# Delta rule: ScalarE issues the transfers of the inverted diagonal blocks, the sync engine only those of the key blocks

## The reference

```python
def step(S, inputs):
    q_t, k_t, v_t, g_t, b_t = inputs
    S = S * jnp.exp(g_t)[..., None, None]
    kv = jnp.einsum('bhk,bhkv->bhv', k_t, S)
    u = b_t[..., None] * (v_t - kv)
    S = S + jnp.einsum('bhk,bhv->bhkv', k_t, u)
    o_t = jnp.einsum('bhk,bhkv->bhv', q_t * scale, S)
    return (S, o_t)
...
_, o = jax.lax.scan(step, S0, (tfirst(q), tfirst(k), tfirst(v), tfirst(g), tfirst(beta)))
...
x = x + _L0_attn_ref(_layernorm(x, axis=-1), ...)
x = x + _L0_ffn_ref(...)
x = x + _L1_attn_ref(...)
x = x + _L1_ffn_ref(...)
```

## Time and profile before

| | |
|---|---|
| median of 3 runs | 2797.41 us (2793.74 to 2800.77) |
| the profiled execution's own time | 2793.88 us |
| its span in the trace | 2792.1 us |
| mean granted clock of TensorE | 0.972 |
| TensorE busy | 94% of the span |
| ScalarE busy | 32% |
| GpSimd busy | 14% |
| the main loop of the delta rule | about 244 to 560 us of the span, a round every 41 to 43 us |

### The profile page before, as it was taken

The page is one execution under the profiler, slowest core; times in us unless marked ns, Lnnn a source line. Parts: engine busy times, 40 slices in busy tenths (PEclk is TensorE's granted clock), DMA queues, the critical chain, the costliest instruction groups (busy, mean ns, idle before and its releaser), DMA issues. The chain is left out here.

```text
span 2792.1 us, 34293 instructions
## 1 busy us (share of the span) xinstructions
PE 2624.4 (94%) x12650; PEld 1956.9 (70%) x12650; DVE 1636.0 (59%) x2426; ACT 886.6 (32%) x1354; POOL 389.1 (14%) x676
## 2 busy tenths in 40 slices
PE   8964889789999999999999989999999989999998
PEld 7844777768888888888888864333333678888886
DVE  7873777574544444455444477777776465655554
ACT  3342443232111111111211125666665322222221
POOL 0018877400000000000000022222210100000000
PEclk9977999989999999999999998999999999999999
DMA  2341331211100000000000014222221000100001
GB/s 92 110 122 41 86 82 40 63 36 33 31 24 23 23 23 23 23 23 23 23 23 23 1 44 76 71 70 72 72 79 37 31 16 32 45 31 15 15 16 46
DMA packets 104218, 122.32 MB, mean 44 GB/s; under 512 B 47454, under 2 KB 80478, under 8 KB 102438
## 3 DMA queue, kind: packets, MB, share of 16 engines
q1 hardware_dynamic: 104102, 120.79, 15.2%
HBM read 88.26 MB, written 24.64 MB: 40 GB/s over the span
## 5 line engine op out<-in xcount | busy, mean ns | idle before, releaser
L2236 DVE TENSOR_REDUCE att_top<-att_scores 128x1 f32<-128x1024 f32 x256 | 312.3, 1224 | 129.3 <-PE att_scores L2396 129.2
L296 DVE TENSOR_TENSOR fp_hidden<-fp_gelu,fp_up 128x512 f32<-128x512 f32 x128 | 88.0, 688 | 440.5 <-PE fp_up L75 377.5
L2109 ACT ACTIVATE att_probs<-att_scores 128x1024 f32<-128x1024 f32 x256 | 262.1, 1024 | 190.5 <-PE att_scores L2421 188.7
L2436 PE MATMUL att_out<-att_probs,att_padded 128*64 128x512 f32 x1024 | 269.5, 616 | 3.0 <-issue 2.8
L278 DVE TENSOR_TENSOR k_stream<-k_stream,fp_down 128x512 f32<-128x512 f32 x256 | 175.2, 685 | 84.1 <-PE fp_down L75 80.7
L356 ACT ACTIVATE fp_gelu<-fp_gate 128x512 f32<-128x512 f32 x128 | 76.3, 596 | 419.7 <-PE fp_gate L75 418.9
L73 PE MATMUL fp_gate<-fp_feat_hi,fp_w_hi 128*128 128x512 f32 x512 | 200.4, 391 | 4.6 <-DVE fp_feat_lo L266 4.6
L75 PE MATMUL fp_gate<-fp_feat_hi,fp_w_lo 128*128 128x512 f32 x512 | 199.9, 391 | 0.0
L74 PE MATMUL fp_gate<-fp_feat_lo,fp_w_hi 128*128 128x512 f32 x512 | 199.9, 390 | 0.0
L73 PE MATMUL fp_down<-fp_w_hi,fp_h_hi 128*128 128x512 f32 x512 | 199.3, 389 | 0.0
L75 PE MATMUL fp_up<-fp_feat_hi,fp_w_lo 128*128 128x512 f32 x512 | 199.2, 389 | 0.0
(11 more groups left out here) (336 smaller groups left out, 5560.5 us busy)
## 6 DMA issues: line engine op xcount, KB each, us to landing
f_early<-codes SPq DMA_DIRECT2D x16, 768.0 KB
f_early<-scales SPq DMA_DIRECT2D x16, 768.0 KB
att_stacks<-rotated SPq DMA_DIRECT2D x96, 128.0 KB
la_values<-w_sparse SPq DMA_DIRECT2D x10, 1024.0 KB, 4.8
f_early<-qkv SPq DMA_DIRECT2D x14, 576.0 KB, 5.6
att_stacks<-rotated SPq DMA_DIRECT2D x96, 64.0 KB
k_stream<-hidden SPq DMA_DIRECT2D x16, 256.0 KB, 4.2
att_stacks<-att_rot_hi SPq DMA_DIRECT2D x64, 64.0 KB
```

Of the source, the lines that this page charges most:

```text
L296: dve.tensor_tensor(hidden[:, c, :], gelu[:, c, :], up_ps[c][:], ALU.mult).then_inc(product_done, 1)
L2109: act.activation(probs[:, tile % PROBS, :], key_bank(tile)[:], ACT.Exp).then_inc(exp_done, 1)
L2236: dve.tensor_reduce(top[g % 2][:, STACK + t:STACK + t + 1], query_bank(tile)[:], AX.XY, ALU.max, negate=True).then_inc(max_done, 1)
L2436: last = pe.matmul(out[rows, :], padded[:, g % 2, t, :], probs[:, t, half * TB:(half + 1) * TB], start=t == 0, stop=t == T - 1)
```

## The change

SP no longer has `give_blocks`; it keeps `take_blocks`, the loads, and `start_base`. The ten DMAs of `give_blocks` stand in ScalarE's queue, at two places: the store of `base_t`, the four into `diag`, and the store of `base_tt` where `turn_blocks(c + 1)` stood (behind `square_outputs(c)`), and the four into `diag_t` behind `copy_off_blocks(c, 2)` of the round that uses them. Sizes, number and kinds of the DMAs stay. `start_base(c + 3)` on SP now waits for the store of chunk c + 1 and for its transposition, nothing else.

```diff
-            def give_blocks(c):
-                sp.wait_ge(zero_done, 3)
-                for base, produced, scratch, out, target, read, done in (
-                        (base_t, base_done, blocks_t, t_out, diag, m_ps, diag_in),
-                        (base_tt, tt_done, blocks_tt, tt_out, diag_t, y_ps, diag_t_in)):
-                    sp.wait_ge(produced, c + 1)
-                    if c:
-                        sp.wait_ge(done, 16 * QUARTERS * c)
-                    sp.dma_start(scratch.rearrange("q i r c -> (q i) r c"), base[base_rows(c), :, :]).then_inc(out, 16)
-                    sp.wait_ge(out, 16 * (c + 1))
-                    if c:
-                        sp.wait_ge(read, FOURS * c)
-                    for q in range(QUARTERS):
-                        at = slice(BASE * q, BASE * (q + 1))
-                        sp.dma_start(target[at, :, at], scratch[q].rearrange("i r c -> r i c")).then_inc(done, 16)
-                if c + 2 < CHUNKS:
-                    start_base(c + 2)
-
...
-            give_blocks(0)
+            sp.wait_ge(t_out, 16)
+            sp.wait_ge(tt_done, 1)
+            start_base(2)
...
-                if c + 1 < CHUNKS:
-                    give_blocks(c + 1)
+                if c + 3 < CHUNKS:
+                    sp.wait_ge(t_out, 16 * (c + 2))
+                    sp.wait_ge(tt_done, c + 2)
+                    start_base(c + 3)
...
+            def take_inverse(c, base, produced, scratch, out, done):
+                act.wait_ge(produced, c + 1)
+                if c:
+                    act.wait_ge(done, 16 * QUARTERS * c)
+                act.dma_start(scratch.rearrange("q i r c -> (q i) r c"), base[base_rows(c), :, :]).then_inc(out, 16)
+
+            def place_inverse(c, scratch, out, target, read, done):
+                act.wait_ge(out, 16 * (c + 1))
+                if c:
+                    act.wait_ge(read, FOURS * c)
+                for q in range(QUARTERS):
+                    at = slice(BASE * q, BASE * (q + 1))
+                    act.dma_start(target[at, :, at], scratch[q].rearrange("i r c -> r i c")).then_inc(done, 16)
+
+            def give_blocks(c):
+                take_inverse(c, base_t, base_done, blocks_t, t_out, diag_in)
+                turn_blocks(c)
+                place_inverse(c, blocks_t, t_out, diag, m_ps, diag_in)
+                take_inverse(c, base_tt, tt_done, blocks_tt, tt_out, diag_t_in)
+
...
-            turn_blocks(0)
+            act.wait_ge(zero_done, 3)
+            give_blocks(0)
...
                 copy_off_blocks(c, 2)
+                place_inverse(c, blocks_tt, tt_out, diag_t, y_ps, diag_t_in)
                 if ahead:
                     square_keys(ahead)
...
                     square_outputs(c)
-                    turn_blocks(c + 1)
+                    give_blocks(c + 1)
```

## The result

The changed kernel takes 2838.25 us (median of 5 runs, 2836.47 to 2839.96), before 2797.41 (5 runs, 2793.54 to 2800.77): a ratio of 1.015, 95% interval 1.0136 to 1.0164, or 41 us slower. The forecast was 2817 us with a range of 2805 to 2826. The direction was right, the size half of what came, and the time lies above the range.

What follows compares the result with a forecast made beforehand. The landing of diag, awaited by TensorE's off_blocks, was taken as the bound. Terms 9.8 + 2.5 + 1.4 + 5.3 + 0.7 = 19.7 us, added to the 2797.41 us median, gave 2817 us; range for 8 in 10: 2805 to 2826 us.

Steps and rivals of the forecast that it cites:

- late store, chunks 1 to 5: Before off_blocks of chunks 1 to 5: ScalarE stores the inverses later than SP did, 9.8 us together.
- What bounds the kernel: In the delta rule, TensorE's off_blocks waits for the DMAs into diag, 23.0 us over chunks 1 to 7.
- The store behind `square_outputs`: ScalarE's queue: store 0.05 us after the second square starts, placing 2.48 later, off_blocks 3.65 after that; 9.8 us in all.
- the rival with issues of 0.05 us: "Not slower": ScalarE issues DMAs in a fraction of SP's 0.46 us; about +4 us, 2801 us; chance 0.12.
- What SP does earlier: Unit matrix and load issued beside the DMAs into diag: 1.0 us each before chunks 0 to 4, 0.3 for chunk 5; 5.3 us.
- the upper bound of 2.5 us: Most that SP's transfers could delay the DMAs into diag per round, from a 512 KB residual landing in 5.0 against 2.5 us.
- much slower: Placing DMAs wait for the load (12.5 us), ScalarE's DMAs for its engine's work (4.5 us): 31 us, 2829 us; chance 0.08.
- The DMAs into `diag_t`: Ahead of square_keys on ScalarE, they delay the squares: 2.5 us over rounds 1 to 5, 1.4 us in round 0.
- The clock: Before chunk 3, TensorE's off_blocks would start at half clock after the longer wait: at most 1.5 us, taken as 0.7.
- the cover for which I took half: ScalarE's copies run beside off_blocks' half-clock products, so only half of at most 1.5 us was counted, 0.7 us.
- The lateness of chunk 6: About 2 us, expected to disappear in TensorE's 8.81 us wait for GpSimd before chunk 7.
- `square_queries` behind the placing DMAs: On ScalarE, square_queries starts 2.3 us later but has cover: costed at nothing, up to 2.3 us in five rounds without it.

Runs made afterwards that it cites:

- e1: Changed kernel, but SP waits until the four DMAs into diag have landed before issuing the unit matrix and the load; 2811.68 us, ratio 1.0059.
- e5: Changed kernel with only the four DMAs into diag_t moved behind square_keys; 2835.59 us, ratio 1.0145.
- e4: Kernel before, with only the store of base_tt and the four DMAs into diag_t issued by ScalarE; 2804.4 us, ratio 1.0034.
- e9: e1 with the store of base_t moved in front of square_outputs; 2796.64 us, ratio 0.9999.
- e11: e6 with 24 extra products in front of TensorE's wait for diag in every round but the first; 2808.35 us, ratio 1.0044.
- e7: Kernel before, all on SP, with the store of base_t in front of the wait for the key blocks' landing; 2792.69 us, ratio 0.9981.
- e10: Kernel before, with only the store of base_t on ScalarE, behind copy_queries and in front of square_outputs; 2791.57 us, ratio 0.9989.
- e12: e6 with 12 extra products in front of TensorE's wait for diag; 2804.13 us, ratio 1.0037.
- e6: e1 with the four DMAs into diag_t moved from in front of square_keys to behind it; 2809.17 us, ratio 1.0045.

## Why the forecast was half the size

Its terms against what the runs gave, for rounds 0 to 5:

| term | forecast | measured | from |
|---|---|---|---|
| late store, chunks 1 to 5 | 9.8 | 9.75 | e1 against before |
| the DMAs into `diag` beside SP's transfers | 5.3 | 26 | after against e1 |
| `diag_t` ahead of the squares of the keys | 3.9 | 5.3 | round 0: 3.9, of which 1.6 at half clock; round 1: about 1.4 (40.3 against 38.9 in e5) |
| half clock behind the longer waits | 0.7 | 5 | what is left of the 6.4 of rounds 1 to 5 without that 1.4 |
| sum | 19.7 | 46 | 45.6 in the spans |

**What bounds the kernel.** Right: the landing of `diag` was on the path, and 31.5 of 45.6 us appear in that wait.

**The store behind `square_outputs`.** Right in each step, and in the lead of the sequencer over the engine. ScalarE issues a DMA in about 0.5 us, so the rival with issues of 0.05 us is out.

**What SP does earlier.** This is the step that failed. "I take 1.0 us each for rounds with a load": it was 4.9 to 5.7 before chunks 1 to 4, 3.9 at chunk 0, and 0.9 in place of 0.3 before chunk 5 (after against e1). The mechanism was named, but the upper bound of 2.5 us was no bound. It came from the earlier trace rows, a residual issued 3 us *behind* a load, when much of that load had moved. The four DMAs now have all 1,344 KB beside them. With the rate of that moment the bound can be worked out: 1,344 KB at 260 GB/s are 5.3 us. A lead of one issue, 0.4 us, counted for nothing, while one of 2 us (e4) protects. The rival "much slower" had the right sign for this term and too little as well: 12.5 us in place of 26. With 2.5 us in five rounds the sum is 26.9 us or 2824, so the range's upper end of 2826 had room for this bound and no more.

**The DMAs into `diag_t`.** The total of 3.9 us was near by accident. The step for rounds 1 to 5 (0.5 us each) is not seen: with normal issues rounds 2 to 5 are as long with the DMAs ahead of the squares of the keys as behind them, in after against e5 (155.6 and 155.9 us). TensorE's half clock, by which `off_blocks` ends 2 us later there, would be a reason. But e9 has these DMAs ahead of the squares too, and its rounds 3 and 5, with `off_blocks` at the full clock, take 37.2 us each, within the 36.8 to 37.7 us of other kernels' rounds with `off_blocks` at the full clock. So the 0.5 us isn't seen at either clock, and why VectorE's lateness costs nothing stays open. Round 0 cost 3.9 us in place of 1.4: one issue of 2.08 us made the squares late by more than forecast, and 1.6 us are products at half clock, of which the forecast had nothing.

**The clock.** Mis-sized too: 0.7 against 5 us, or 6.6 with that of round 0. I took chunk 3 alone as a change, since the other rounds "have it already". They had it at little cost: five rounds of the kernel before take only 1.6 us more than those of e11, which never leaves the full clock in them. Chunk 3 itself cost 1.7 us (38.95 against 37.23 us), more than the 1.5 called the most. Behind waits of 5 to 10 us `off_blocks` takes 5.1 to 5.5 us in four of the five rounds instead of 4.2 to 4.6, and the cover for which I took half did not hold.

**The rest.** The lateness of chunk 6 disappeared in the wait for GpSimd, which shrank from 8.81 to 6.99 us, as forecast. `square_queries` behind the placing DMAs cost 0.5 us a round at most, and perhaps nothing: they are as late in e11, whose rounds are nearly as short as the one that the kernel before has at the full clock (37.5 to 37.7 us against 37.2 in round 3).

## What to carry to other kernels

When a queue is relieved, ask what it issues next and which transfer on the path that lands beside: here the small transfers took as long as all bytes in flight with them, whichever queue held them, and bulk loads 2 us behind them, or held until they had landed, did little harm. The price of contention was here the bytes over the measured rate, not the nearest slow row, which had a different overlap. Before moving DMAs to another engine, look for the wait in the old queue that makes them late; one store moved ahead of one wait (e7) brought 3 to 5 us where the whole change cost 41. And look for the next limit before you price it: here that was GpSimd.

## What had not been expected of the hardware

- Four DMAs of 48 KB landed up to 7.3 us after their issue instead of 2.2, beside 1,344 KB issued within 0.8 us in another queue, at 220 to 310 GB/s in all. In one queue, behind 1,152 KB, issuing the four also took 3.65 us instead of 1.85.
- A single issue of a DMA on ScalarE or SP sometimes takes 1.2 to 2.1 us instead of 0.5, in round 0 on ScalarE in nine of ten traces. The cause stays open.
- TensorE's granted clock: the 24 matmuls of `off_blocks` took 2.94 us or less behind every wait up to 1.82 us, and 4.3 to 5.5 us behind every wait from 3.65 us on. In between both occur: 2.94 us behind 2.15 and 3.35 us in e7, 2.44 us in e10 and 2.62 us in e9, but 4.3 and 4.6 us behind 1.83 and 2.00 us in e4. What decides there was not found. Filling part of a wait with extra products (e12 against e6) took 6 us off five rounds of the traces.
